# Attention probabilities: from TensorE transposes to VectorE block transposes and a DMA exchange

## The chip, the cores and the metric

One core of one Trainium2 chip. The metric is the device time of the program in microseconds, here the median of three runs; lower is better.

## The reference

One transformer layer on x of 2048 tokens by 512. With 16 heads, NOPE = 128, ROPE = 64, a latent of 128 and causal softmax over all 2048 tokens:

```
xn = layernorm(x)
q = xn @ wq.T                       # per head: 128 plain, 64 rotary
kv_lat, k_pe = split(xn @ wkv_a.T)  # 128 and 64, shared by the heads
kv = rmsnorm(kv_lat, w)
scores = (q_nope @ wkv_b_k @ kv.T + rope(q_pe) @ rope(k_pe).T) * 192**-0.5, causal
out = softmax(scores) @ kv @ wkv_b_v @ wo.T
result = x + out + ternary_linear(xn) + bias
```

## The kernel before, in words

`build_prepare` normalises x, makes the keys (Kn_h, Kn_l, Kp), the values (V_h, V_l), the weights Wq, Wp, Wv of each head, and stores these, the transposed x and the residual in memory. Every float32 operand of a product is split in a high part (a copy rounded to fp32r) and a low part (the difference), and a product of two such operands is three matmuls.

`build_attention` runs over 4 chunks of 512 queries (j) and in each over 16 heads. A chunk j has 4(j+1) units per head; a unit is one score tile of 128 queries by up to 512 keys. A step works on the scores of a head (cur), on the probabilities of the head before (prev) and on the query of the next (nxt). The order on every engine is written out by hand in its `step`.

- TensorE: `scores` (L967, five matmuls of 512 columns, and a mask on the diagonal), `transposes` (L990: for one tile of 128 keys up to four 128x128 transposes of float32 into a ring of three PSUM tiles, L1000), `values` (L1004, three matmuls for one tile of keys, two units behind the transposes), `project_rotary` (12 matmuls, every second head), `project_latent` (12), `project_out` (L1016, 12, at the step's end).
- VectorE: `copy_scores` (L1062: scaled copy of the scores to SBUF with their maximum), `split_tile` (L1077: low part of the transposed probabilities), `rotate`, `split_query`, `split_output`, `accumulate`.
- ScalarE: `exp_row` (L1146, one row of 128 queries at a time), `high_tile` (L1155: high part of the transposed probabilities), `high_output`, `high_query`, `high_rotary`. In a step `high_output` (L1206) stands ahead of the last `exp_row` (L1208).
- GpSimd: `add_rotary` and two halves of `low_rotary` a head.
- SyncE: the loads of Wq, Wp, Wv for coming heads, of xT, tables and residual for the next chunk, and the store of a finished chunk. cosT, sinT and acc have two buffers each, Wq and Wv two.

The probabilities of two heads (probs, 4 rows of 2048 each) are kept.

Of the kernel before, what the change touches and what calls it, by code (L numbers as in the profile page):

```python
# [32 lines left out]
H = 16  # L33
# [18 lines left out]
PT_RING = 3  # L52


def need(eng, sem, value):

    if isinstance(value, int) and value <= 0:
        return
    eng.wait_ge(sem, value)

def heads_before(pos):
    j, m, p = pos
    return H * j + 2 * m + p


def tiles_before(pos):

    j, m, p = pos  # L70
    return QB * H * (j * (j + 1) // 2) + QB * (j + 1) * (2 * m + p)


def rows_before(pos):
    return QB * heads_before(pos)


def pairs_before(pos):
    j, m, p = pos
    return (H // 2) * j + m  # L80


def tiles_of(pos):
    return QB * (pos[0] + 1)


def first_of_chunk(pos):
    return isinstance(pos[1], int) and pos[1:] == (0, 0)


def first_row(pos, k):

    return max(0, k - QB * pos[0])


def rotary_unit(nxt, units):

    if nxt[2]:
        return None
    return units * 3 // 4 if first_of_chunk(nxt) else units // 2 - (1 if units == QB else 0)  # L100


def walk(nc, engine, step):


    def two_steps(j, m):
        step((j, m, 1), (j, m, 0), (j, m + 1, 0))
        step((j, m + 1, 0), (j, m, 1), (j, m + 1, 1))

    for j in range(NCH):  # L110
        step((j, 0, 0), (j - 1, H // 2 - 1, 1) if j else None, (j, 0, 1))
        if j == 0:

            two_steps(0, 0)
        with nc.Fori(0 if j else 1, H // 2 - 1, engines=[engine]) as m:
            two_steps(j, m)
        step((j, H // 2 - 1, 1), (j, H // 2 - 1, 0), (j + 1, 0, 0) if j + 1 < NCH else None)
    step(None, (NCH - 1, H // 2 - 1, 1), None)


def build_prepare(nc, t, keep, stored):
# [4 lines left out]
    with ExitStack() as ctx:  # L126
# [9 lines left out]
        ident, xT, residual = keep["ident"], keep["xT"], keep["acc0"]  # L136
        Wq, Wp, Wv = keep["Wq"], keep["Wp"], keep["Wv"]
# [137 lines left out]
        def _(sp):  # L275
# [51 lines left out]
            rounds(ENG.SP, round_)  # L327

# [462 lines left out]
def build_attention(nc, t, keep, stored):  # L791
    with ExitStack() as ctx:
# [9 lines left out]
        xT, Wq, Wp, Wv = (keep[k] for k in ("xT", "Wq", "Wp", "Wv"))  # L802

        cosT = [keep["cosT"], sb("cosT1", [P, CW])]
        sinT = [keep["sinT"], sb("sinT1", [P, CW])]
        acc = [keep["acc0"], sb("acc1", [P, QB, D])]
# [4 lines left out]
        probs = [sb(f"probs{i}", [P, QB, S]) for i in range(2)]  # L811
        pT_h = [sb(f"pT_h{i}", [P, CW], F32R) for i in range(PT_RING)]
        pT_l = [sb(f"pT_l{i}", [P, CW], F32R) for i in range(PT_RING)]
        o_h = sb("o_h", [P, CW], F32R)
        o_l = sb("o_l", [P, CW], F32R)
        rot_cos = sb("rot_cos", [P, CW])
        rot_sin = sb("rot_sin", [P, CW])
        rotated = sb("rotated", [P, CW])
        part_max = [sb(f"part_max{i}", [P, QB, NCH]) for i in range(2)]
# [3 lines left out]
        ident, ident16, mask = keep["ident"], keep["ident16"], keep["mask"]  # L823
        Kn_h, Kn_l, Kp = (keep[k] for k in ("Kn_h", "Kn_l", "Kp"))
        V_h, V_l = (keep[k][:, :].rearrange("p (n c) -> p n c", c=RANK) for k in ("V_h", "V_l"))

        p_score = [ps(f"p_score{i}") for i in range(2)]
        p_tr = [ps(f"p_tr{i}") for i in range(PT_RING)]
        p_out = ps("p_out")
# [3 lines left out]
        p_result = p_tr + [p_out]  # L833

        xT_in = sem("xT_in")
        tables_in = sem("tables_in")
        wq_in = [sem(f"wq_in{i}") for i in range(2)]
        wp_in = sem("wp_in")
        wv_in = [sem(f"wv_in{i}") for i in range(2)]
# [491 lines left out]
```

## Time and profile before

| What | us |
|---|---|
| median of 3 runs (1955.99 to 1956.75) | 1956.49 |
| the profiled execution | 1956.91 |
| its span | 1955.1 |
| TensorE busy | 1898.6 |
| VectorE busy | 1271.2 |
| ScalarE busy | 889.5 |
| GpSimd busy | 313.3 |

How to read it: one execution was recorded; the span goes from its first to its last instruction. Busy time adds up instructions; a share near 100% marks the engine that has no free time. The chain that ended last goes back from the last instruction, at each step to what released it. PE is TensorE's matmuls, PEld its weight loads, DVE VectorE, ACT ScalarE, POOL GpSimd, SP SyncE; PEclk is TensorE's granted clock as a part of full speed. A stretch is given in us from the span's start. The preparation takes about the first 180 us, the chunks end near 427, 797, 1308 and 1955 us.

### The profile page before, as it was taken

The page shows a single profiled execution, that of the slowest core. Times are in us where ns is not written, and L with a number is a line of the kernel's source. Part 1 is how long each engine was busy: PE and PEld are TensorE (multiplying, and loading weights), DVE is VectorE, ACT ScalarE, POOL GpSimd, SP SyncE. Part 2 cuts the span into 40 slices and gives each one's busy share as a digit, 9 for nine tenths or more (in the row PEclk, how much of TensorE's full clock was granted, in tenths as well). Part 3 has the DMA queues.
Part 4 walks back from the last instruction along what each step waited for, and adds up shares of the span by engine and source line. Part 5 has one row for each costly group of instructions (what it writes and reads, how often), then busy time and mean ns, then how long its engine had stood idle before and what let it go on. Part 6 is the DMA issues. An engine that isn't in the chain of part 4 may idle for free.

```text
span 1955.1 us, 32275 instructions
## 1 busy us (share of the span) xinstructions
PE 1898.6 (97%) x10350; PEld 1586.6 (81%) x10350; DVE 1271.2 (65%) x3025; ACT 889.5 (45%) x1646; POOL 313.3 (16%) x313
## 2 busy tenths in 40 slices
PE   6998999999999999999999999999999999999998
PEld 5887787778888888888888888878888888888886
DVE  4764676766666666666766666666666666666665
ACT  4554444444444444444444444444443444434443
POOL 4773212211111111011100111011010110101100
PEclk9888999999999999999999999999999999999999
DMA  6993322232111112210111101111000110001000
GB/s 207 367 333 149 119 97 81 101 140 87 54 64 54 55 69 101 87 44 35 51 43 43 43 32 54 72 57 45 22 32 32 43 32 21 32 32 43 11 11 22
DMA packets 53077, 147.46 MB, mean 75 GB/s; under 512 B 4835, under 2 KB 17380, under 8 KB 51493
## 3 DMA queue, kind: packets, MB, share of 16 engines
q1 hardware_dynamic: 52208, 145.71, 21.5%
q10 hardware_dynamic: 820, 1.15, 0.2%
q8 instruction: 26, 0.43, 0.1%
q14 instruction: 23, 0.18, 0.0%
HBM read 112.23 MB, written 34.60 MB: 75 GB/s over the span
## 4 chain that ended last, share of the span: by engine, by line
PE 81%; DVE 4%; issue 3%; POOL 2%; ACT 0%; DVEq 0%; POOLq 0%; ACTq 0%
PE p_score L983 31%; PE p_out L1012 18%; PE p_tr L1000 12%; PE p_lat L963 7%; PE p_tr L1023 6%; PE p_rot L963 4%; DVE rot_sin L1095 2%; PE p_out L1023 2%; DVE probs L1068 1%; PE p_score L987 1%; POOL qp_l L1234 1%; POOL qp_l L1237 1%; POOL rotated L1223 1%; DVE pT_l L1080 0%; DVE rot_cos L1091 0%
## 5 line engine op out<-in xcount | busy, mean ns | idle before, releaser
L1160 ACT ACTIVATE pT_h<-p_tr 128x512 fp32r<-128x512 f32 (+3 forms) x640 | 339.4, 532 | 790.4 <-PE p_tr L1000 788.3
L1068 DVE TENSOR_SCALAR_CACHE_REDUCE probs<-p_score 128x512 f32<-128x512 f32 (+3 forms) x640 | 388.3, 607 | 168.8 <-PE p_score L983 109.6
L1080 DVE TENSOR_TENSOR pT_l<-p_tr,pT_h 128x512 fp32r<-128x512 f32 (+3 forms) x640 | 390.2, 610 | 159.9 <-ACT pT_h L1160 153.5
L1000 PE MATMUL p_tr<-ident,probs 128*128 128x128 f32 x2176 | 343.1, 273 | 0.0
L1151 ACT ACTIVATE probs<-probs,neg_max 128x128 f32<-128x128 f32 (+15 forms) x256 | 307.5, 1201 | 70.5 <-DVE neg_max L1074 69.3
L1000 PEld LDWEIGHTS p_tr<-ident,probs 128*128 128x128 f32 x2176 | 260.5, 140 | 52.6 <-issue 0.2
L1012 PE MATMUL p_out<-pT_h,V_h 128*128 128x512 f32 (+3 forms) x640 | 274.7, 429 | 6.8 <-DVE pT_l L1080 6.8
L983 PE MATMUL p_score<-Kn_h,q_h 128*128 128x512 f32 (+3 forms) x640 | 241.4, 377 | 3.3 <-DVE q_l L1102 3.3
L983 PE MATMUL p_score<-Kp,qp_h 128*128 128x512 f32 (+3 forms) x640 | 234.5, 366 | 8.8 <-POOL qp_l L1237 8.8
L1012 PE MATMUL p_out<-pT_h,V_l 128*128 128x512 f32 (+3 forms) x640 | 234.9, 367 | 0.0
L1012 PE MATMUL p_out<-pT_l,V_h 128*128 128x512 f32 (+3 forms) x640 | 233.5, 365 | 0.0
L983 PE MATMUL p_score<-Kp,qp_l 128*128 128x512 f32 (+3 forms) x640 | 233.4, 365 | 0.0
L983 PE MATMUL p_score<-Kn_h,q_l 128*128 128x512 f32 (+3 forms) x640 | 233.4, 365 | 0.0
L983 PE MATMUL p_score<-Kn_l,q_h 128*128 128x512 f32 (+3 forms) x640 | 232.1, 363 | 0.0
L1223 POOL TENSOR_TENSOR rotated<-rot_cos,rot_sin 128x512 f32<-128x512 f32 x32 | 41.1, 1286 | 1112.1 <-DVE rot_sin L1095 1112.1
L963 PE MATMUL p_lat<-xT,Wq 128*128 128x512 f32 x768 | 203.2, 397 | 0.0
L963 PEld LDWEIGHTS p_lat<-xT,Wq 128*128 128x128 f32 x768 | 138.2, 188 | 21.8
L983 PEld LDWEIGHTS p_score<-Kp,qp_h 128*128 128x128 f32 x640 | 120.8, 189 | 29.3 <-POOL qp_l L1237 11.2
L983 PEld LDWEIGHTS p_score<-Kn_h,q_h 128*128 128x128 f32 x640 | 120.8, 189 | 27.3 <-DVE q_l L1102 5.3
L1234 POOL TENSOR_TENSOR qp_l<-rotated,qp_h 64x512 fp32r<-64x512 f32 x64 | 82.4, 1288 | 362.3 <-ACT qp_h L1179 362.3
L983 PEld LDWEIGHTS p_score<-Kn_l,q_h 128*128 128x128 f32 x640 | 121.1, 189 | 22.6
L1117 DVE SCALAR_TENSOR_TENSOR acc<-p_tr,inv_sum,acc 128x512 f32<-128x512 f32 x192 | 132.6, 745 | 8.6 <-PE p_tr L1023 2.8
(138 smaller groups left out, 2622.6 us busy)
## 6 DMA issues: line engine op xcount, KB each, us to landing
Wq<-wq_scr SPq DMA_DIRECT2D x62, 512.0 KB, 3.3
Wv<-wv_scr SPq DMA_DIRECT2D x62, 512.0 KB, 3.3
Wp<-wp_scr SPq DMA_DIRECT2D x31, 512.0 KB, 3.2
wq_scr<-Wq SPq DMA_DIRECT2D x16, 512.0 KB, 5.9
wv_scr<-Wv SPq DMA_DIRECT2D x16, 512.0 KB, 5.8
xT_scr<-xT SPq DMA_DIRECT2D x3, 2048.0 KB, 9.9
xT<-xT_scr SPq DMA_DIRECT2D x3, 2048.0 KB, 7.9
x_in<-in_x SPq DMA_DIRECT2D x4, 1024.0 KB, 7.6
```

The lines of the kernel that those rows point to most:

```text
L963: mm = pe.matmul(out, weights[:, w, it, :], xT[:, x, it, :], start=(it == 0 and k == 0), stop=(it == IT - 1 and k == 2))
L983: mm = pe.matmul(out[:, 0:width], q[p][:, rows], kk[:, keys], start=(k == 0), stop=(k == 4 and b < j))
L1000: mm = pe.transpose(p_tr[k % PT_RING][:, i * P:(i + 1) * P], probs[p][:, i, k * P:(k + 1) * P], ident[:, :])
L1012: mm = pe.matmul(p_out[:, cols], v[:, k, :], pt[r][:, cols], start=(k == 0 and a == 0), stop=(last and a == 2))
L1023: mm = pe.matmul(out[:, :], o[:, rows], Wv[p][:, w, :], start=(k == 0), stop=(k == 2))
L1068: dve.tensor_scalar(probs[p][:, i, b * CW:b * CW + width], p_score[u % 2][:, 0:width], SCALE, LOWEST, ALU.mult, ALU.max, accum_out=part_ma ...
L1080: dve.tensor_tensor(pT_l[r][:, cols], p_tr[r][:, cols], pT_h[r][:, cols].bitcast(F32), ALU.subtract).then_inc(pT_split, 1)
L1117: dve.scalar_tensor_tensor(out=a[:, i, :], in0=p_result[i][:, :], scalar=inv_sum[p][:, i:i + 1], in1=a[:, i, :], op0=ALU.mult, op1=ALU.add ...
L1151: act.activation(probs[p][:, i, 0:width], probs[p][:, i, 0:width], ACT.Exp, bias=neg_max[p][:, i:i + 1], scale=1.0, accum_out=row_sum[p][: ...
L1160: act.activation(pT_h[r][:, cols], p_tr[r][:, cols], ACT.Copy).then_inc(pT_high, 1)
L1223: pool.tensor_tensor(rotated[:, :], rot_cos[:, :], rot_sin[:, :], ALU.add).then_inc(rot_added, 1)
L1234: pool.tensor_tensor(qp_l[p][0:ROPE, :], rotated[own, :], qp_h[p][own, :].bitcast(F32), ALU.subtract).then_inc(qp_ready, 1)
```

## The change

The transposes on TensorE and the splits behind them (`transposes`, `high_tile`, `split_tile`) are gone. In their place:

- VectorE transposes a row of probabilities in blocks of 32x32, up to 8 key tiles in one instruction (`turn_row`), into `turned`; SyncE moves the blocks between the partitions with 16 DMAs a head (`exchange`), each from 32 partitions to 32 partitions, 4(j+1) x 512 bytes in each; ScalarE makes the high parts in groups of two key tiles (`high_group`, a ring of three), GpSimd the low parts, in place (`low_group`). There is one `turned` and one `pT`.
- Step g has the scores of head g, the exchange, groups and values of head g-1 (its last row is turned in step g), the query of head g+1, and output projection and accumulation of head g-2. Except in chunk 0 the values begin at unit 6 (LEAD) and are spread over the units up to the last but one; in chunk 0 they all stand behind the scores.
- The score ring has three PSUM tiles instead of two, the results two; probs keeps three rows. Wq, Wv, cosT, sinT and acc are single. The loops of the sequencers are written out.
- SyncE's order in a step: exchange(g-1), load_q(g+2), load_v(g-1), load_rotary(g+3) in odd steps; tables and xT in step 14 of a chunk, store and load of acc in step 1.

```
+SCORE_RING = 3
+ROW_RING = 3
+HIGH_RING = 3
+LEAD = 6
+def values_by(cur, prev, u):
+    units, tiles = tiles_of(cur), tiles_of(prev)
+    if chunk_of(cur) == 0 or u < LEAD:
+        return 0
+    return min(tiles, -(-tiles * (u - LEAD + 1) // (units - 1 - LEAD)))
+def groups_ahead(cur, prev, u):
+    ahead = min(u + 2, tiles_of(cur) - 1)
+    return (values_by(cur, prev, ahead) + 1) // 2
+def row_due(cur, i):
+    j = chunk_of(cur)
+    return (i + 1) * (j + 1) + (1 if j else 0)
...
+        turned = sb("turned", [P, 4, NT, QB, 32])
+        pT = sb("pT", [P, 4, NT, QB, 32], F32R)
+        pT_h = [sb(f"pT_h{i}", [P, 4, 2, QB, 32], F32R) for i in range(HIGH_RING)]
...
+            def exchange(g):
+                tiles = tiles_of(g)
+                sp.wait_ge(blocked, QB * (g + 1))
+                need(sp, pv_done, tiles_before(g))
...
+                for a in range(4):
+                    for r in range(4):
+                        sp.dma_start(pT[32 * a:32 * (a + 1), r, 0:tiles, :, :].bitcast(F32),
+                                     turned[32 * r:32 * (r + 1), a, 0:tiles, :, :]).then_inc(exchanged, 16)
...
-            def transposes(pos, k):
...
+            def values(g, k):
+                n = groups_before(g) + k // 2
+                if k == 0:
+                    need(pe, o_split, g)
+                if k % 2 == 0:
+                    pe.wait_ge(p_low, n + 1)
...
+                need(pe, accumulated, n - 1)
+                out, rows = p_result[n % 2], slice(i * P, (i + 1) * P)
```

TensorE's step:

```
+                for u in range(units):
+                    if g < HEADS:
+                        scores(g, u)
+                    if u == 0 and g % 2 and g + 1 < HEADS:
+                        project_rotary(g + 1)
+                    if u < QB and g >= 2:
+                        project_out(g - 2, u)
+                    if u < IT and g + 1 < HEADS:
+                        project_latent(g + 1, u)
+                    if 1 <= g < HEADS:
+                        for k in range(done, values_by(g, g - 1, u)):
+                            values(g - 1, k)
```

VectorE's new operation and its step:

```
+            def turn_row(g, i):
+                row, tiles = QB * g + i, QB * chunk_of(g) + i + 1
+                dve.wait_ge(exped, row + 1)
+                if i == 0:
+                    need(dve, exchanged, 256 * g)
+                for first in range(0, tiles, 8):
...
+                    last = dve.transpose(turned[:, :, t8, i, :].rearrange("p a t q -> p t a q"),
+                                         rows.rearrange("p (t a q) -> p t a q", a=4, q=32))
+                last.then_inc(blocked, 1)
...
+                for u in range(units):
+                    if g < HEADS:
+                        copy_scores(g, u)
+                    if 1 <= g <= HEADS and u == (1 if chunk_of(g - 1) else 0):
+                        turn_row(g - 1, QB - 1)
+                    if g >= 2 and u >= 1 and u <= QB - 1:
+                        accumulate(g - 2, u - 1)
...
+                    if u == min(5, units - 1) and g + 1 < HEADS:
+                        split_query(g + 1)
+                    for i in range(QB - 1):
+                        if g < HEADS and u == row_due(g, i):
+                            turn_row(g, i)
+                if 1 <= g <= HEADS:
+                    split_output(g - 1)
+                    invert(g - 1)
```

ScalarE's new operation and its step:

```
+            def high_group(g, k):
...
+                if k == 0:
+                    act.wait_ge(exchanged, 256 * (g + 1))
+                need(act, pv_done, 2 * (n - HIGH_RING + 1))
...
+                for u in range(units):
+                    if 1 <= g < HEADS:
+                        for k in range(done, groups_ahead(g, g - 1, u)):
+                            high_group(g - 1, k)
...
+                    if g < HEADS and (u + 1) % (chunk_of(g) + 1) == 0:
+                        exp_row(g, u // (chunk_of(g) + 1))
+                    if u == 4 and g + 1 < HEADS:
+                        high_query(g + 1)
+                        high_rotary(g + 1)
...
+                if 1 <= g <= HEADS:
+                    high_output(g - 1)
```

GpSimd's step, and the clearing ahead of its first:

```
+                for k in range(groups):
+                    low_group(g - 1, k)
+                    if k == 1 and g + 1 < HEADS:
+                        low_rotary(g + 1, groups_before(g - 1) + 2)
...
+            pool.memset(turned[:, :, :, :, :], 0.0).then_inc(cleared, 1)
```

## Rows read from the trace of the kernel before

**Rows 1.** The page: busy time of the engines; the chain that ended last, by line.
```profile
PE 1898.6 (97%) x10350; PEld 1586.6 (81%) x10350; DVE 1271.2 (65%) x3025; ACT 889.5 (45%) x1646; POOL 313.3 (16%) x313
...
PE p_score L983 31%; PE p_out L1012 18%; PE p_tr L1000 12%; PE p_lat L963 7%; PE p_tr L1023 6%; PE p_rot L963 4%; DVE rot_sin L1095 2%; PE p_out L1023 2%; DVE probs L1068 1%; PE p_score L987 1%; POOL qp_l L1234 1%; POOL qp_l L1237 1%; POOL rotated L1223 1%; DVE pT_l L1080 0%; DVE rot_cos L1091 0%
```

**Rows 2.** Busy time in one stretch: us, then PE, PEld, DVE, ACT, POOL, PEclk, DMA share, GB/s.
```profile
1308.00:1922.00 614.00, 613.09 (x3304) 511.64 (x3303) 396.88 (x928) 275.16 (x420) 45.08 (x35) 1.00 0.09 31
```

**Rows 3.** The chain in order of time, rotary projections: start us, us, what.
```profile
287.25 2.78 PE p_rot L963 x12
...
316.01 2.78 PE p_rot L963 x12
...
488.61 2.76 PE p_rot L963 x12
...
534.01 2.76 PE p_rot L963 x12
...
880.18 2.75 PE p_rot L963 x12
...
943.38 2.75 PE p_rot L963 x12
...
1415.36 2.75 PE p_rot L963 x12
...
1496.98 2.75 PE p_rot L963 x12
```

**Rows 4.** Timeline of PE, chunk 3, first products of two units: start us, us, what.
```profile
1751.08 0.40 PE L983 MATMUL p_score<-Kn_h,q_h 128*128 128x512 f32 x1
...
1753.38 0.40 PE L983 MATMUL p_score<-Kn_h,q_h 128*128 128x512 f32 x1
```

**Rows 5.** Groups by line and form: count, busy us, mean ns, idle before.
```profile
L1000 PE MATMUL p_tr<-ident,probs 128*128 128x128 f32 x2176 | 343.1, 273 | 0.0
...
L1080 DVE TENSOR_TENSOR pT_l<-p_tr,pT_h 128x512 fp32r<-128x512 f32 x448 | 309.3, 691 | 139.1 <-ACT pT_h L1160 134.7
...
L1234 POOL TENSOR_TENSOR qp_l<-rotated,qp_h 64x512 fp32r<-64x512 f32 x64 | 82.4, 1288 | 362.3 <-ACT qp_h L1179 362.3
...
L1080 DVE TENSOR_TENSOR pT_l<-p_tr,pT_h 128x256 fp32r<-128x256 f32 x64 | 27.1, 423 | 10.7 <-ACT pT_h L1160 10.5
...
L1151 ACT ACTIVATE probs<-probs,neg_max 128x1024 f32<-128x1024 f32 x16 | 18.3, 1144 | 1.3 <-DVE neg_max L1074 1.3
...
L336 POOL TENSOR_TENSOR wkb_l<-wkb,wkb_h 128x256 fp32r<-128x256 f32 x16 | 12.3, 768 | 25.4 <-ACT wkb_h L413 25.4
```

**Rows 6.** Timeline of SyncE's queue, chunk 0: start us, us of the issue, what.
```profile
180.60 0.34 SPq L871 DMA_DIRECT2D Wp<-wp_scr  x1
...
197.90 0.43 SPq L894 DMA_DIRECT2D cosT<-in_cosT  x1
198.38 0.43 SPq L895 DMA_DIRECT2D sinT<-in_sinT  x1
```

**Rows 7.** DMA issues: count, KB each, median us to landing.
```profile
Wq<-wq_scr SPq DMA_DIRECT2D x62, 512.0 KB, 3.3
...
xT<-xT_scr SPq DMA_DIRECT2D x3, 2048.0 KB, 7.9
```

**Rows 8.** DMA of 23.93 to 24.48 us, when wqp (64 partitions) lands.
```profile
DMA packets 71, 0.13 MB, mean 231 GB/s; under 512 B 9, under 2 KB 9, under 8 KB 71
```

**Rows 9.** Timelines of DVE and ACT at the end of a chunk-3 step.
```profile
1759.06 0.69 DVE L1068 TENSOR_SCALAR_CACHE_REDUCE probs<-p_score 128x512 f32<-128x512 f32 x1 [1.08 <-PE p_score L987]
...
1761.76 0.69 DVE L1106 TENSOR_TENSOR o_l<-p_out,o_h 128x512 fp32r<-128x512 f32 x1 [1.58 <-ACT o_h L1166]
...
1761.62 2.00 ACT L1151 ACTIVATE probs<-probs,neg_max 128x2048 f32<-128x2048 f32 x1
```

**Rows 10.** Busy time in two stretches of the preparation; columns as in rows 2.
```profile
64.00:68.00 4.00, 2.35 (x17) 1.94 (x14) 3.90 (x6) 0.91 (x2) 2.96 (x3) 0.88 1.08 361
68.00:72.00 4.00, 4.00 (x19) 3.81 (x19) 0.73 (x2) 2.77 (x6) 1.91 (x2) 0.50 1.02 350
```

More of the change, by code:

```diff
@@ L51, with chunk_of, tiles_of, tiles_before @@
 LOWEST = -3.0e38
-PT_RING = 3
-def need(eng, sem, value):
[L57 to L118, printed above, removed]
+SCORE_RING = 3
+ROW_RING = 3
+HIGH_RING = 3
+LEAD = 6
+HEADS = NCH * H
+def need(eng, sem, value):
+    if value > 0:
+        eng.wait_ge(sem, value)
+def chunk_of(g):
+    return g // H
+def tiles_of(g):
+    return QB * (chunk_of(g) + 1)
+def tiles_before(g):
+    j = chunk_of(g)
+    return QB * H * (j * (j + 1) // 2) + QB * (j + 1) * (g - H * j)
+def groups_of(g):
+    return tiles_of(g) // 2
+def groups_before(g):
+    return tiles_before(g) // 2
+def opens_chunk(g):
+    return g % H == 0
+def values_by(cur, prev, u):
[9 more added lines that the diff above has]
+    return (i + 1) * (j + 1) + (1 if j else 0)
 def build_prepare(nc, t, keep, stored):
@@ L855, in build_attention @@
         exped = sem("exped")
[L856 removed]
+        p_high = sem("p_high")
         o_high = sem("o_high")
@@ L1013, in values @@
+                if k % 2 == 0:
+                    pe.wait_ge(p_low, n + 1)
+                last = k == tiles_of(g) - 1
+                i = slice(max(0, k - QB * chunk_of(g)), QB)
+                high, low = pT_h[n % HIGH_RING][:, :, k % 2, i, :], pT[:, :, k, i, :]
+                for a, (v, pt) in enumerate(((V_h, high), (V_l, high), (V_h, low))):
+                    mm = pe.matmul(p_out[:, :, i, :], v[:, k, :], pt, start=(k == 0 and a == 0),
                                    stop=(last and a == 2))
@@ L1022, in project_out, with step @@
                 for k, (o, w) in enumerate(((o_h, 0), (o_h, 1), (o_l, 0))):
-                    mm = pe.matmul(out[:, :], o[:, rows], Wv[p][:, w, :], start=(k == 0), stop=(k == 2))
+                    mm = pe.matmul(out[:, :], o[:, rows], Wv[:, w, :], start=(k == 0), stop=(k == 2))
                 mm.then_inc(out_projected, 1)
-            def step(cur, prev, nxt):
-                units = tiles_of(cur) if cur else tiles_of(prev)
-                tiles = tiles_of(prev) if prev else 0
+            def step(g):
+                units = tiles_of(g) if g < HEADS else QB
@@ L1029, in step @@
                 done = 0
                 for u in range(units):
-                    if cur:
-                        scores(cur, u)
-                    if u < tiles:
-                        transposes(prev, u)
-                    if u >= 2 and u - 2 < tiles:
-                        values(prev, u - 2)
-                        done = u - 1
-                    if nxt and u == rotary_unit(nxt, units):
-                        project_rotary(nxt)
-                order = ["q", "v", "q", "v", "q", "q"] if units == QB else ["q", "v", "v", "q", "q", "q"]
@@ L1043, in step @@
-                it = 0
-                for what in order:
-                    if what == "v" and done < tiles:
-                        values(prev, done)
-                        done += 1
-                    if what == "q" and nxt:
-                        project_latent(nxt, it)
-                        it += 1
-                if prev:
-                    for i in range(QB):
-                        project_out(prev, i)
-            project_rotary((0, 0, 0))
+                    if g < HEADS:
+                        scores(g, u)
@@ new lines, in step @@
+                    if u == 0 and g % 2 and g + 1 < HEADS:
[7 more added lines that the diff above has]
+                            values(g - 1, k)
+                            done = k + 1
+                if 1 <= g <= HEADS:
+                    for k in range(done, tiles_of(g - 1)):
+                        values(g - 1, k)
@@ L1251, in build @@
+            pool.wait_ge(cleared, 1)
+            add_rotary(0)
+            low_rotary(0, 0)
+            for g in range(HEADS + 2):
+                step(g)
 def build(nc, t):
```

430 lines of the change are left out of this document (197 added, 233 removed).

## The prediction

> **What bounds the kernel now.** I read the page first: TensorE is busy 97% of the 1955.1 us span, VectorE 65%, ScalarE 45%, GpSimd 16%, and in the chain that ended last, TensorE's scores are 31% of the span, its values 18%, and the transposes of the probabilities (L1000) 12% [rows 1]. Then the stretch of the last chunk: 613.09 of 614 us busy at full clock, DMA share 0.09 [rows 2]. So TensorE is the bound, and whatever leaves it is gained as long as nothing takes its place. The chain in order of time gives the length of two heads as the distance between two rotary projections: 28.76, 45.40, 63.20 and 81.62 us in chunks 0 to 3 [rows 3], so 14.4, 22.7, 31.6 and 40.8 us a head, 109.5 together; 16 of each are 1752 us of the span. A full unit (five score products, four transposes, three value products) takes 2.30 us from one start to the next [rows 4]; twelve products of that size in a row take 2.75 us [rows 3], 0.23 each, so eight are 1.84 and the four transposes the other 0.46: 0.11 us each.
>
> **What is removed.** 2176 transposes [rows 5] at 0.11 us are 239 us of TensorE; 6.4 us a head in chunk 3 (58 of them), 4.6, 2.9 and 1.1 in the others. VectorE loses 640 splits (390 us), ScalarE 640 copies out of PSUM.
>
> **What is added, and its prices.**
> - VectorE turns each row. Two tensor forms give 0.423 us for 256 and 0.691 for 512 elements [rows 5], 1.05 ns an element over 0.15: 1.22 us for 1024, 2.4 us for a row of 2048. No transpose on VectorE is in the trace; from below, the same at no fixed cost (2.1), from above twice as much. I take 2.4; the upper end adds some 6 us over one head of each chunk, 100 us in all.
> - ScalarE copies groups of two key tiles, 1024 elements: 1.14 us, as the exponential of that width [rows 5].
> - GpSimd now makes the low parts, which VectorE made: 0.768 us for 256 and 1.288 for 512 elements give 2.03 ns an element, 2.33 us for 1024; the last group of a head is half, 1.3. Beside it stay two rotary lows of 1.29 [rows 5] and, every second head, an add of the same length. In chunk 3 that is 7 × 2.34 (with the wait) + 1.3 + 2.6 = 20.3 us behind the exchange.
> - SyncE issues 16 DMAs a head, 1, 2, 3 or 4 MiB in all. Issues behind one another stand 0.48 us apart, of which the issue itself is 0.43; alone it takes 0.34 [rows 6]; I take 0.43 (0.34 to 0.48): 6.9 us before the last has started, whatever its size. 512 KB land in 3.3 and 2048 KB in 7.9 us [rows 7]: 342 GB/s over 1.8 us. But these reach all 128 partitions, each exchange DMA reads 32 and writes 32. The nearest row is a load to 64 partitions, at 231 GB/s [rows 8]. I take 230, nearest in shape; 342 is the upper end, and the lower 156, if a quarter of the partitions falls behind a half as the half does behind the whole (231/342).
>
> The Trainium skill, SBUF — State Buffer, section Door 1: The DMA port swizzle, says that 32 partitions reach 8 of 16 ports, some 218 GB/s, and that two DMAs to different halves do not add up; by it the sum below would be some 35 us larger; it gives 64 partitions no more than 32, and the row's 231 GB/s is near its figure.
>
> So the exchange X (issue or bytes, whichever is longer, plus 1.8) is 8.7, 10.9, 15.5 and 20.0 us in chunks 0 to 3.
>
> **What it costs depends on what stands in series with it.** Nothing is doubled: one turned tile, one pT. The exchange of head g−1 can't start before its last row is turned, early in step g; turn_row(g, 0), in the middle of VectorE's queue, waits for it, and the score copies behind it, so the score ring stops TensorE; and the values need GpSimd's lows, which need it too. I follow chunk 3 from the last score product of a step:
> - Copy and maximum 1.1 us, exponential of 2048 elements 2.1, then high_output, which is queued behind that exponential, 0.6, then split_output 0.7 [rows 9]: only at 4.7 may TensorE project out. That, three latent products and scores(1) take 2.5 us, the copy 0.75, and VectorE, in whose queue turn_row(g−1, 3) stands behind this copy, ends it at 8.0 + 2.4: D = 10.6 us.
> - X = 20.0. TensorE has done all score units up to 6 by about 18 us and waits.
> - From the landing: high group 1.2, low group 2.4, and then TensorE's values (0.69 us a full tile) and scores (1.15) as the lows come: low 2 stands behind the rotary lows at 10.9, and with 13 us of values and scores behind, TensorE ends scores(15) 26.4 us after the landing.
> The head is 10.6 + 20.0 + 26.4 = 57.0 us against 40.8. The others by the same walk:
> - Chunk 2 (12 units): a shorter exponential and row make D = 9.6; behind the landing two high groups, the query's and the rotary's copies and GpSimd's lows (3.6, 5.9, rotary to 8.5, then 10.8, 13.2, 15.5, 16.8 us) decide, with values 8 to 11 and the last two scores behind them: 20.2. 9.6 + 15.5 + 20.2 = 45.3 for 31.6.
> - Chunk 1 (8 units): D = 7.8; all eight values stand in unit 6, the fourth high group waits for the first two values (ring of three), the rotary copies stand behind it, so the rotary lows end at 10.4, the last low at 14.0, and two values and scores(7) follow: 16.0. 7.8 + 10.9 + 16.0 = 34.7 for 22.7.
> - Chunk 0 (4 units): turn_row(g, 0) is in unit 1, so behind the landing come VectorE's last two units with accumulates and, every second head, rotary (3.2 or 4.6 us to the last maximum), the exponential 0.9, the query's copy 0.6, a high group 1.2, lows and rotary lows 6.2 (scores of the next head wait for these), then score, copy and the turn of the last row 1.9, and in odd steps 0.8 more for the add: 15.1 with the waits. 15.1 + 8.7 = 23.8 for 14.4.
> Sum 160.8 for 109.5: 51.3 × 16 = 821 us more. So the transposes' 239 us are inside and paid over.
>
> Loads of Wq, Wv and Wp now stand behind the exchange on SyncE. They are for the next step and land in 3.3 us [rows 7]; a step leaves 15 us or more after the exchange, so I count nothing; without that cover, 3 us a head. Single acc, tables and xT cost at chunk ends up to 10 us each, against a last step whose values and outputs are shorter without transposes; the clearing of turned, once, is 8192 elements, at most 16.6 us by GpSimd's slope, partly beside the first rotary: 0 in sum, bounds ±30.
>
> **The clock.** After a stretch with TensorE busy 2.35 of 4 us, its granted clock was 0.50 (1.2 GHz) through the next 4 us, which it worked without a gap [rows 10]. The change makes a gap of over 10 us a head. At 1.2 GHz some 3 us can be lost behind each; most of it lies under GpSimd's lows. Bounds 0 and 192 us, taken 1 us a head: 64.
>
> The sum is made against the execution's own 1956.9 us (span 1955.1), which is 0.4 us above the median of the runs: 1957 + 821 + 64 = 2840 us.
>
> **Rivals.**
> 1. The exchange runs as fast as a transfer over all partitions, 342 GB/s: X = 8.7, 8.7, 11.0, 14.1, and 38.7 × 16 + 64 = 683: 2640 us. For it: SBUF to SBUF takes no memory access outside, and the sources alternate. Against it: [rows 8]. 0.20.
> 2. The clock stays down behind the gap through the whole tail, where TensorE works only as lows come. At 1.2 GHz its 19.8 us of values and scores in chunk 3 become 39.6 for 26.4, and 26 for 20.2 in chunk 2: 19 × 16 = 304 more, 3080 us. Against it: once it is the slower one it has no gaps, and where the trace shows none for long the clock is whole [rows 2]. 0.14.
> 3. On the other side: the exchange is hidden, as the late values intend. Its place is the wait of turn_row(g, 0); it decides below X = 3.8 us in chunk 3 (37.0 + X = 40.8) and is fully hidden near 2 us, below which TensorE sets the end: 1957 − 239, and back 2.3, 1.9, 1.5 us a head for the output split behind the exponential (91 us): 1810 us. It needs 4 MiB at over 1000 GB/s, or my series is not one. 0.04, and 0.01 for ending within the measurement.
> 4. The change doesn't keep what it says: the transposes do leave, but "late in a step" is no cover if everything before unit 6 takes 18 us and the landing comes at 30. That is inside the forecast.
>
> The Trainium skill, TensorE: Matmul & The Clock Gate, section HAM oscillation, describes a kernel that is thrown back to the low clock at every wait for a DMA; here that is rival 2 where it lasts, and the 64 us of my sum where not.
>
> **How the numbers follow.** The forecast (exchange at 190 to 260 GB/s, 2740 to 2980) has 0.61. With rivals 1 and 2 in part the range is 2570 to 3040: below it lie the fast exchange with cheap issues and rival 3, above it the clock that stays down, and 156 GB/s (some 310 us more). Over 0.2% (4 us, about what a measurement of this kernel can tell) slower 0.95, faster 0.04, same 0.01.
>
> **What would show it.** Right: TensorE busy at some 60%, one long idle time a head, ended in the waits by p_low, o_l or q_l; VectorE's longest wait for the exchange before a transpose; SyncE's 16 issues some 0.4 us apart in each head; GpSimd busy about 1000 us; periods near 48, 69, 91 and 114 us for two heads; the last exchange of a head landing 20 us after its first issue in chunk 3. Wrong: DMA moving over 300 GB/s within an exchange (rival 1), clock near 0.5 in the value stretches (2), or values beginning at unit 6 with no wait (3). A transpose on VectorE of 2.4 us for 1024 elements would put the end about 100 us later.

## The result, and the profile after

The changed kernel takes 3007.3 us (median of four runs, 2998.91 to 3010.15), against 1956.62 for the kernel before: 1.536 times as long, with a 95% interval of 1.533 to 1.540. The forecast was 2840 (2570 to 3040), slower. So the sign and the range held; the move was forecast as +883 us and is +1051, 168 more. The profiled execution took 3010.1 us, with a span of 3007.9.

The page, first engines and TensorE's granted clock in 40 slices:

```profile
PE 1929.9 (64%) x8174; PEld 1539.6 (51%) x8174; DVE 1209.3 (40%) x2769; ACT 857.6 (29%) x1326; POOL 1000.7 (33%) x634
...
PEclk9987677688877877878797888878878888788877
```

Against [rows 1] TensorE has 2176 instructions fewer, and is busy 64% of the time for 97%. It is no longer the bound, and no other engine is: the next, VectorE, is busy 40%. That is the picture of work in series. The waits say which series (what waited <- for what: us in total, times, longest):

```profile
POOL pT L1244 <- ACT pT_h L1165: 1221.5, 73, 41.9
...
PE p_out L1006 <- POOL pT L1244: 853.1, 113, 22.8
...
ACT pT_h L1165 <- DMA pT<-turned: 626.6, 49, 25.2
...
DVE turned L1073 <- DMA pT<-turned: 359.0, 48, 16.1
```

Read upwards from the DMA: ScalarE's first copy of a head waits for the exchange (49 times 12.8 us), GpSimd for ScalarE, TensorE for GpSimd. In chunk 0, where ScalarE does not wait, VectorE does. One head of chunk 3, put together from the timelines of SyncE, ScalarE, GpSimd and TensorE (start us, us, what; in brackets the idle time before it and what ended it):

```profile
2599.14 14.99 SPq L876 DMA_DIRECT2D pT<-turned  x16
2614.16 1.17 SPq L882 DMA_DIRECT2D Wq<-wq_scr  x1
...
2621.29 1.06 ACT L1165 ACTIVATE pT_h<-pT 128x1024 fp32r<-128x1024 f32 x1 [16.90 <-DMA pT<-turned]
...
2622.42 2.36 POOL L1244 TENSOR_TENSOR pT<-pT,pT_h 128x1024 fp32r<-128x1024 f32 x1 [40.00 <-ACT pT_h L1165]
...
2624.93 0.77 PE L1006 MATMUL p_out<-pT_h,V_h 128*128 128x512 f32 x1 [18.03 <-POOL pT L1244]
...
2630.59 13.07 POOL L1244 TENSOR_TENSOR pT<-pT,pT_h 128x1024 fp32r<-128x1024 f32 x6
```

The 16 issues alone take 15 us, and the first copy starts 22.15 us after the first issue; TensorE stands still for 18 us, up to the first low part. GpSimd is busy from 2622.42 to 2643.66 almost without a gap: that is the series of low parts behind the landing. The same head in stretches of 5 us (columns as in [rows 2]):

```profile
2600.00:2605.00 5.00, 5.00 (x26) 4.17 (x26) 2.45 (x8) 1.78 (x2) 0.00 (x0) 1.00 0.97 213
2605.00:2610.00 5.00, 1.90 (x9) 1.25 (x7) 1.65 (x5) 0.00 (x0) 0.00 (x0) 0.96 1.04 215
2610.00:2615.00 5.00, 0.00 (x0) 0.00 (x0) 0.00 (x0) 0.00 (x0) 0.00 (x0) 0.50 1.01 210
2615.00:2620.00 5.00, 0.00 (x0) 0.00 (x0) 0.00 (x0) 0.00 (x0) 0.00 (x0) 0.50 1.01 203
2620.00:2625.00 5.00, 0.07 (x1) 0.10 (x1) 2.14 (x3) 3.65 (x5) 2.36 (x1) 0.50 0.59 208
2625.00:2630.00 5.00, 5.00 (x15) 4.13 (x16) 1.61 (x6) 2.48 (x4) 4.51 (x3) 0.50 0.00 0
```

For ten microseconds no engine works at all and the DMA engines move 203 to 210 GB/s at a share of 1.0: they are full, at that rate. The Trainium skill, SBUF — State Buffer, section Door 1: The DMA port swizzle, gives 218 GB/s for 32 partitions; the trace agrees, at 5% less.

The length of a head is the distance of the output split (L1106 before, L1100 after) from one head to the next, X the time from the first issue of an exchange to its last landing; both are means over the same 12 heads in the middle of each chunk:

| chunk | before | after | forecast | X after | X forecast |
|---|---|---|---|---|---|
| 0 | 14.39 | 27.47 | 23.8 | 11.6 | 8.7 |
| 1 | 22.74 | 39.23 | 34.7 | 12.0 | 10.9 |
| 2 | 31.68 | 47.96 | 45.3 | 17.3 | 15.5 |
| 3 | 40.55 | 60.55 | 57.0 | 22.4 | 20.0 |
| sum | 109.4 | 175.2 | 160.8 | 63.3 | 55.1 |

Sixteen of each: 65.8 × 16 = 1053 us, the whole of the move.

### The profile page after: what moved, and what is told of

The parts are those of the page before. It is cut to its first block and busy times, and to the rows that moved or that the text cites. A ratio compares the mean times of both kernels' runs of the same rounds, so it can differ in the third digit from the quotient of the medians.

```text
span 3007.9 us, 24655 instructions
## 1 busy us (share of the span) xinstructions
PE 1929.9 (64%) x8174; PEld 1539.6 (51%) x8174; DVE 1209.3 (40%) x2769; ACT 857.6 (29%) x1326; POOL 1000.7 (33%) x634
## 5 line engine op out<-in xcount | busy, mean ns | idle before, releaser
L1244 POOL TENSOR_TENSOR pT<-pT,pT_h 128x1024 fp32r<-128x1024 f32 x320 | 682.8, 2159 | 1228.1 <-ACT pT_h L1165 1221.5
L1006 PEld LDWEIGHTS p_out<-pT_h,V_h 128*128 128x128 f32 x640 | 156.1, 244 | 928.5 <-issue 741.1
L1165 ACT ACTIVATE pT_h<-pT 128x1024 fp32r<-128x1024 f32 x320 | 301.9, 967 | 893.3 <-DMA pT<-turned 626.6
L1073 DVE STREAM_TRANSPOSE turned<-probs 128x1024 f32<-128x1024 f32 (+7 forms) x384 | 341.8, 916 | 359.1 <-DMA pT<-turned 359.0
L1018 PE MATMUL p_result<-Wv,o_h 128*128 128x512 f32 x512 | 194.4, 464 | 172.7 <-DVE acc L1114 93.1
L1006 PE MATMUL p_out<-pT_h,V_l 128*128 128x512 f32 (+3 forms) x640 | 283.9, 444 | 0.0
L1006 PE MATMUL p_out<-pT,V_h 128*128 128x512 f32 (+3 forms) x640 | 281.2, 439 | 0.0
L1018 PEld LDWEIGHTS p_result<-Wv,o_h 128*128 128x128 f32 x512 | 90.9, 209 | 213.1 <-DVE acc L1114 108.1
L1114 DVE SCALAR_TENSOR_TENSOR acc<-p_result,inv_sum,acc 128x512 f32<-128x512 f32 x256 | 188.7, 739 | 3.1 <-PE p_result L1018 2.4
L1006 PEld LDWEIGHTS p_out<-pT,V_h 128*128 128x128 f32 x640 | 156.0, 244 | 27.5
```

Source lines behind the costliest of these rows:

```text
L1006: mm = pe.matmul(p_out[:, :, i, :], v[:, k, :], pt, start=(k == 0 and a == 0), stop=(last and a == 2))
L1018: mm = pe.matmul(out[:, :], o[:, rows], Wv[:, w, :], start=(k == 0), stop=(k == 2))
L1073: last = dve.transpose(turned[:, :, t8, i, :].rearrange("p a t q -> p t a q"), rows.rearrange("p (t a q) -> p t a q", a=4, q=32))
L1114: dve.scalar_tensor_tensor(out=acc[:, i, :], in0=p_result[(QB * g + i) % 2][:, :], scalar=inv_sum[g % 2][:, i:i + 1], in1=acc[:, i, :], op ...
L1165: act.activation(pT_h[n % HIGH_RING][:, :, :, i, :].rearrange("p r t i q -> p r t (i q)"), pT[:, :, tiles, i, :].bitcast(F32).rearrange("p ...
L1244: pool.tensor_tensor(low, low.bitcast(F32), high.bitcast(F32), ALU.subtract).then_inc(p_low, 1)
```

## The experiments

Each ran once, with a profile, beside the kernel before at 1955.95 to 1956.89 us; four repeats of the changed kernel spread over 11 us, so differences under some 12 us are not read. All edits are to the changed kernel. Four head lengths in a row are those of chunks 0 to 3, and these and every X are means over the 12 heads of the table; the texts put down before the runs took X from one head of each chunk (11.9, 12.6, 17.4 and 22.1).

**One DMA of the sixteen.** The exchange moves a sixteenth; the rest of pT keeps zeros, so fifteen sixteenths of the probabilities are left out of the values.

```
-                for a in range(4):
-                    for r in range(4):
-                        sp.dma_start(pT[32 * a:32 * (a + 1), r, 0:tiles, :, :] ...
+                sp.dma_start(pT[0:32, 0, 0:tiles, :, :] ... turned[0:32, 0, 0:tiles, :, :]) ...
```

> Leaves out fifteen of the sixteen DMAs of every exchange (only the block from partitions 0 to 31 to partitions 0 to 31 is moved; the rest of pT stays cleared); all waits stay. Series theory (the whole exchange stands in every head's chain): the exchange takes 11.9, 12.6, 17.4 and 22.1 us in chunks 0 to 3 of the changed kernel, and one DMA about 2.4, so each head loses 9.5, 10.2, 15.0 and 19.7 us, 16 times 54.4 = 870 us of 3007: about 2140 us, some 50 less if TensorE's clock stays up. Rival (VectorE's transposes or GpSimd's lows are the bound and the exchange lies beside them): above 2700 us.

Measured 2361.38 us; heads 22.44, 31.89, 36.24 and 44.3, 40.3 less in sum. SyncE's and ScalarE's timelines:

```profile
2070.01 0.51 SPq L874 DMA_DIRECT2D pT<-turned  x1
...
2075.15 1.04 ACT L1162 ACTIVATE pT_h<-pT 128x1024 fp32r<-128x1024 f32 x1
```

X is 2.0, 2.3, 2.6 and 3.0 us now, so it falls by 9.6, 9.8, 14.6 and 19.4 us; the heads fall by 5.0, 7.3, 11.7 and 16.3 us, that is 2.4 to 4.6 us less in each chunk. In chunk 3 the first copy starts 5.1 us after the issue, behind an exponential, with no wait for a DMA. So the first few microseconds of an exchange lie beside work that has to be done anyway, in every chunk, and below that other work sets the head. 646 us of the 1051 go with the fifteen DMAs, together with what their wait did to TensorE's clock (a mean of 0.895 now, for 0.813); the 405 that are left (2361 against 1956) come with no exchange worth the name. I had expected X to count whole and missed by some 220 us.

**Sixteen small DMAs.** All are issued, but each moves one tile of keys, 16 KB in every chunk; the other key tiles of the probabilities are left out.

```
-                        sp.dma_start(pT[32 * a:32 * (a + 1), r, 0:tiles, :, :] ...
+                        sp.dma_start(pT[32 * a:32 * (a + 1), r, 0:1, :, :] ...
```

> All sixteen DMAs of an exchange, but each moves one key tile only (512 bytes of each of 32 partitions; the rest of pT stays cleared). Issue theory (SyncE's issues of 0.65 us each set the exchange where the data are few): the exchange is 16 times 0.65 plus 1.5 = 11.9 us in every chunk, so the others lose 0.7, 5.5 and 10.2 us a head, 262 us: 2745 us. Rival (bytes alone at some 205 GB/s): a quarter of a MiB is moved in under 2 us, the exchange takes about 3.5 us, 50 us less over the four chunks' heads: 2200 us.

Measured 2724.57 us; heads 27.22, 38.17, 42.21, 49.56. SyncE's and ScalarE's timelines in chunk 3:

```profile
2438.01 10.01 SPq L876 DMA_DIRECT2D pT<-turned  x16
...
2449.26 1.06 ACT L1165 ACTIVATE pT_h<-pT 128x1024 fp32r<-128x1024 f32 x1 [5.05 <-DMA pT<-turned]
```

With hardly any bytes the 16 issues take 10 us, 0.63 each, and the landing follows 11.25 us behind the first. Chunk 0 is as slow as with all bytes (27.22 for 27.47), chunk 3 is 11 us faster. So issues bound chunk 0 and nearly all of chunk 1, bytes chunks 2 and 3. In these two X falls by 5.9 and 10.9 us and the head by 5.8 and 11.0: at this size the exchange counts whole.

**Alternating halves.** The order of the 16 DMAs changes, so that neighbours write to and read from different halves of the partitions.

```
-                for a in range(4):
-                    for r in range(4):
+                for s in range(4):
+                    for q in range(4):
+                        a, r = (0, 2, 1, 3)[q], (0, 2, 1, 3)[(q + s) % 4]
```

> The same sixteen DMAs in another order: neighbours write, and read, alternately partitions 0 to 63 and 64 to 127. Theory of the halves (a transfer to 32 partitions reaches half of what SBUF can take, and a queue of transfers to both halves gets more): the exchange in chunks 2 and 3 falls from 17.4 and 22.1 us to the issue's 12 to 13, 14 us less, 16 times: about 2785 us. Rival (the rate is that of each DMA by itself, whatever stands beside it): no change, 2995 to 3020 us.

Measured 2951.01 us, neither of the two; X is 20.5 in chunk 3 and 15.4 in chunk 2, 1.9 us less in both, and so are the heads (58.67 and 46.10). In stretches within an exchange:

```profile
2560.00:2565.00 5.00, 0.55 (x3) 0.13 (x1) 0.29 (x2) 0.00 (x0) 0.00 (x0) 0.91 1.02 233
2565.00:2570.00 5.00, 0.00 (x0) 0.00 (x0) 0.00 (x0) 0.00 (x0) 0.00 (x0) 0.50 1.02 231
```

The rate rises from some 207 to 232 GB/s, an eighth: the order counts, but sixteen transfers in a queue do not overlap enough to make up one over all partitions, which the loads of [rows 7] show at 342.

**Last row turned first.** VectorE turns the last row of the head before it copies any score of the step.

```
                 for u in range(units):
+                    if 1 <= g <= HEADS and u == 0:
+                        turn_row(g - 1, QB - 1)
                     if g < HEADS:
                         copy_scores(g, u)
-                    if 1 <= g <= HEADS and u == (1 if chunk_of(g - 1) else 0):
-                        turn_row(g - 1, QB - 1)
```

> VectorE turns the last row of head g-1 as the first thing of step g, ahead of both score copies, instead of behind the second. Series theory: the exchange starts earlier by the two copies and the wait for the second scores, 4.9, 3.6, 2.9 and 0.3 us in chunks 3 to 0, 11.7 times 16 = 187 us less: 2820 us. Rival (the start of the exchange is not on the path that sets the end): 3000 us or more, since the copies that free the score ring come later.

Measured 2825.11 us, 182 less; heads 27.31, 36.23, 43.84, 56.33. The turn no longer stands behind two copies and the wait for the second scores, and the first issue comes 2.9, 4.2 and 4.4 us sooner behind the last exponential in chunks 1 to 3. The heads are 3.0, 4.1 and 4.2 us shorter, so all of that is gained: the start of the exchange is on the path.

**Two issuing queues.** ScalarE issues the half that writes partitions 64 to 127, behind its first work of a step.

```
-                for a in range(4):
+                for a in range(0, 2):
...
+            def exchange_part(g):
+                act.wait_ge(blocked, QB * (g + 1))
+                need(act, pv_done, tiles_before(g))
+                for a in range(2, 4):
+                    for r in range(4):
+                        act.dma_start(pT[32 * a:32 * (a + 1), r, 0:tiles, :, :] ...
```

> The changed kernel, with the 16 DMAs of an exchange issued half by SyncE and half by ScalarE. It tells the cost of issuing from the cost of the bytes with all bytes kept. Theory (issues at 0.65 us each bound chunks 0 and 1, bytes at 207 GB/s bound chunks 2 and 3): first issue to landing falls from 11.9 to about 7 us in chunk 0, from 12.6 to 11.9 in chunk 1, and stays at 17.4 and 22.1 in chunks 2 and 3; 6 us over the four chunks, times 16 is 96: about 2910 us. Rival a (the rate belongs to one queue, two carry twice as much): chunk 3 near 14 us, together 23 us, 2640 us. Rival b (issues hold each other up across queues): no change, 2995 to 3015 us.

Measured 2901.02 us. X is 6.9, 11.4, 16.9 and 21.6 us in chunks 0 to 3, forecast 7, 11.9, 17.4 and 22.1. The timelines of SyncE and ScalarE in chunk 3:

```profile
2495.30 14.15 SPq L876 DMA_DIRECT2D pT<-turned  x8
...
2495.30 15.58 ACTq L1166 DMA_DIRECT2D pT<-turned  x8
2510.98 1.68 ACT L1154 ACTIVATE probs<-probs,neg_max 128x1664 f32<-128x1664 f32 x1 [23.62 <-issue]
```

The queues run side by side, but with bytes in the way eight issues take as long as sixteen did: 1.8 and 1.9 us each. An issue's length in chunks 2 and 3 is the DMA engines' pace, handed back to the queue. The Trainium skill, DMA: Bandwidth & Descriptors, section Rules for kernel authors, says that spreading DMAs over issuing engines only saves issue time; the run agrees: of its 106 us 80 lie in chunk 0 (22.48 us a head for 27.47), where issues were the bound. X is also 0.4 to 0.8 us shorter in chunks 1 to 3; why was not separated. The second queue has a price on ScalarE, whose exponential of the next row stands behind the issues.

**The clock held.** Idle products into the output bank that the values overwrite, placed where TensorE waits for the first low part.

```
                     need(pe, o_split, g)
+                    for _ in range(16 * chunk_of(g)):
+                        pe.matmul(p_out[:, :, :, :], Kn_h[:, 0:P], Kn_l[:, 0:CW], start=True, stop=True)
```

> The changed kernel, with 16, 32 and 48 idle products (128x512, into the output bank that the values overwrite) a head in chunks 1, 2 and 3, placed where TensorE waits for the first low parts; they take 3.7, 7.4 and 11 us at full clock, less than the waits of 8.6, 13.2 and 18.0 us there. They keep TensorE's clock from falling and measure what its fall costs. Theory (my term of 1 us a head, on 48 heads): about 2950 us. Rival a (the slow values lie wholly under GpSimd's low parts): 2995 to 3010. Rival b (the clock costs 3 us a head): about 2860 us, with the values behind the wait at 0.23 us each instead of 0.43.

Measured 3025.65 us, above all that was expected. In chunk 3 the 48 products left a gap of 7 us, and the values began at 0.43 us each, at a granted clock of 0.50 again. So the run tells little of the clock, and a longer one followed, `(0, 32, 50, 72)[chunk_of(g)]` in place of `16 * chunk_of(g)`:

> The changed kernel with more idle products than e6_warm (32, 50 and 72 a head in chunks 1 to 3: 7.4, 11.5 and 16.6 us at full clock, against waits of 8.6, 13.2 and 18.0 us), since in that run 48 left a gap of 7 us in chunk 3 and the values began at 0.43 us each, at a granted clock of 0.50. Theory (now the fall is gone, but its cost was under GpSimd's lows): values at 0.23 us each from the first, time 3000 to 3035, as e6_warm. Rival (the fall of the clock costs what I forecast, and e6_warm did not prevent it): about 2950.

Measured 3016.23 us; the mean granted clock rises from 0.813 to 0.913. The page's clock row:

```profile
PEclk9887776799999899999999999999999999999998
```

From the ninth slice on, chunk 1 and later, it is 9 tenths or more in nearly every one, for the 7s and 8s of the changed kernel. One head of it in stretches, the values starting at 2619.20 (columns as in [rows 2]):

```profile
2610.00:2615.00 5.00, 5.00 (x24) 4.14 (x23) 0.00 (x0) 0.00 (x0) 0.00 (x0) 1.00 0.99 201
2615.00:2620.00 5.00, 3.33 (x15) 2.42 (x14) 2.79 (x4) 4.31 (x6) 2.75 (x2) 1.00 0.48 186
2620.00:2625.00 5.00, 4.33 (x21) 3.19 (x19) 1.04 (x6) 4.33 (x5) 4.65 (x4) 1.00 0.00 0
2625.00:2630.00 5.00, 2.64 (x6) 2.12 (x7) 0.61 (x2) 0.06 (x1) 5.00 (x3) 0.74 0.01 2
```

The clock holds over the landing and the first values take 0.23 us each, yet the time does not fall. TensorE, faster now, runs into GpSimd's low parts (POOL 4.65 and 5.00 of 5 us busy) and waits there, and the values behind that wait take 0.43 us each again:

```profile
2627.36 0.74 PE L1008 MATMUL p_out<-pT_h,V_h 128*128 128x512 f32 x1 [2.49 <-POOL pT L1246]
```

The heads show what the total hides: 27.39, 38.13, 48.62 and 61.94 us, so 1.1 less than in the changed kernel in chunk 1, and 0.7 and 1.4 more in chunks 2 and 3. In chunks 2 and 3 the last low part ends 17.2 and 22.6 us behind the landing, for 17.1 and 22.3 without the idle products: their pace there is GpSimd's, whatever TensorE's speed, and behind later waits TensorE loses what it had gained: the last score ends 0.7 us later in both. In chunk 1 they end 1.2 us sooner, because ScalarE's fourth high group waits for the first two values. The exchange is also longer beside the idle products, 23.0 us for 22.4 in chunk 3, and 22.9 with fewer of them; why is open. So this run moves the fall of the clock to a later wait; what a clock that never falls would be worth, it doesn't measure.

**Output first.** On top of the last row turned first (2825 us), ScalarE copies the output's high part before the last exponential of the step, in chunks 1 to 3.

```
+                    early = 1 <= g < HEADS and chunk_of(g) > 0
+                    if early and u == units - 1:
+                        high_output(g - 1)
                     if g < HEADS and (u + 1) % (chunk_of(g) + 1) == 0:
                         exp_row(g, u // (chunk_of(g) + 1))
...
-                if 1 <= g <= HEADS:
+                if 1 <= g <= HEADS and not early:
                     high_output(g - 1)
```

> The kernel with the last row turned first in a step (2825 us), and besides, in chunks 1 to 3, the output's high part made by ScalarE ahead of the last row's exponential, so that TensorE and VectorE needn't wait for it behind that exponential. Theory (the exchange's start sets the head: it comes 1.1 us earlier, as copy and split of the output leave the path between exponential and turn): 48 x 1.1 = 53 us, about 2770 us. Rival a (TensorE's own early work is in the series too): the 2.2 us of both count, about 2720. Rival b: hidden, 2815 to 2830.

Measured 2771.46 us, 54 less for 53 forecast; heads 27.12, 35.25, 42.70, 55.15, about 1.1 less each in chunks 1 to 3. Only what stands between the last exponential and the first issue counts.

**All four together** (turned first, output first, two queues, halves alternated in both).

> The four edits that give the exchange less to wait for together: last row turned first, output's high part ahead of the exponential, issues on two queues, and partition halves alternated in both. If their gains add (182 + 53 + 96 + 56 us): about 2620 us. Theory (exchange stays in series with the lows, so still far above the kernel before): 2600 to 2720 us. Rival (shorter exchanges fall under the 4 us of other work that the kernel with one DMA showed, so the gains overlap): 2720 to 2780 us.

Measured 2626.33 us. The plain addition of what each gave (182, 54, 106 and 56 us) makes 2609, so the gains add but for 17 us; the 2620 expected had 96 us for the two queues. Heads 22.49, 34.07, 40.90, 53.55. It is the fastest variant of the changed kernel that leaves nothing out, and still 670 us above the kernel before.

**Low parts split.** VectorE makes every second low part, with a semaphore of its own; it stands in VectorE's queue at the end of the unit before the one whose values need it.

```
+                dve.tensor_tensor(low, low.bitcast(F32), high.bitcast(F32), ALU.subtract).then_inc(p_low_v, 1)
...
-                    pe.wait_ge(p_low, n + 1)
+                    pe.wait_ge(p_low_v if n % 2 else p_low, n // 2 + 1)
...
                 for k in range(groups):
+                    if k % 2 == 0:
                         low_group(g - 1, k)
```

> The changed kernel, with every second low part made by VectorE (1.2 us each by its slope) and the others by GpSimd (2.36 us each). It measures how much of a head is GpSimd's series behind the landing. Theory (the series is the bound): in chunk 3 four lows and two rotary lows instead of eight and two leave TensorE's own 19.8 us as the bound, 3.8 us less a head; by the same walk about 5, 4 and 2.4 us less in chunks 2, 1 and 0; together 15 x 16 = 243: about 2760 us. Rival a (high parts and TensorE at its low clock take the place of the lows): 2890 to 2960. Rival b (VectorE's lows delay the copies of the scores as much as they give): 2990 to 3020.

Measured 3057.25 us, 50 slower: neither the theory nor rival a, and beyond rival b. Heads 27.27, 40.11, 49.18, 61.71. VectorE's and GpSimd's timelines in chunk 3:

```profile
2671.20 1.22 DVE L1084 TENSOR_TENSOR pT<-pT,pT_h 128x1024 fp32r<-128x1024 f32 x1
2676.53 2.76 DVE L1084 TENSOR_TENSOR pT<-pT,pT_h 128x1024 fp32r<-128x1024 f32 x1
...
2671.59 3.09 POOL L1263 TENSOR_TENSOR pT<-pT,pT_h 128x1024 fp32r<-128x1024 f32 x1 [1.21 <-ACT pT_h L1184]
2675.81 2.40 POOL L1263 TENSOR_TENSOR pT<-pT,pT_h 128x1024 fp32r<-128x1024 f32 x1 [1.13 <-ACT pT_h L1184]
```

VectorE's part starts first at 2671.20 and takes 1.22 us, up to 2672.42; GpSimd's, begun at 2671.59, ends at 2674.68, 2.26 us after that end. The other way round GpSimd's ends at 2678.21 and VectorE's, begun at 2676.53, 1.08 us after. So the two did not run beside each other, they took turns; over all its 96 parts of this width VectorE needs 2.15 us on average. The Trainium skill, SBUF — State Buffer, section Who interferes with whom, states this as a lock between a VectorE instruction with two inputs in SBUF and a reading GpSimd one; the trace agrees. On top of that VectorE's part stands behind score copies and a turn of 2.1 us, and GpSimd now waits, 1.21 and 1.13 us in these rows, for ScalarE's high parts, which wait for the values three groups back (237 us in this kernel, 266 in the changed one). In this head the last low part ends 22.1 us after the first high part began (in the changed kernel 22.4), but over 12 heads it ends 19.2 and 23.5 us behind the landing in chunks 2 and 3, for 17.1 and 22.3: halving GpSimd's share made the series longer. Which of the turns and the two queues weighs how much was not separated.

**Low parts split, and the clock held.**

> e9_low_split and e10_warm_long together: with fewer lows on GpSimd nothing should hide the slow products. Theory (the clock's cost was hidden by the lows, some 2.5 us a head where it shows): some 120 us below e9_low_split. Rival (the clock costs nothing there either): within 20 us of e9_low_split.

Measured 2996.79 us, 60 below the split alone: half of what I expected and outside the rival. Heads 27.40, 38.60, 47.78, 61.29: the clock held over the landing is worth 1.5 and 1.4 us a head in chunks 1 and 2 and 0.4 in chunk 3.

**All five.**

> The kernel with the four edits for the exchange (2626 us), and every second low part on VectorE. Theory (exchange and lows are in series, so the gains add): 2626 less what e9_low_split gives (forecast 243), about 2390 us, still some 430 us above the kernel before, of which 22 to 40 us a head of exchange and turning in series are the cause. Rival (the two shorten each other's cover): 2450 to 2600.

Measured 2675.83 us, 50 above the four together, where I had expected about 2390, and 2450 to 2600 as the rival. The split costs the same there as alone.

## Why the prediction was right, and where it was off

The direction is right for the reason given: with one buffer the exchange, the turn before it and the lows behind it stand in series. That the time lies in the range owes something to luck: 3007 is above the band of 2740 to 2980 that had 0.61, and 33 us below the upper end, in a part of the range that was meant for rivals 1 and 2 in part. What brought the time there are three terms that the sum had too small: the issue, the rate, and the tail of chunk 1. By the parts of a head, in us, forecast in brackets (D from a head's last score to the first issue, the tail from the landing to the next head's last score; in chunk 0, where the parts lie otherwise, the head without X):

| chunk | D | X | tail |
|---|---|---|---|
| 0 | together 15.9 (15.1) | 11.6 (8.7) | |
| 1 | 7.6 (7.8) | 12.0 (10.9) | 19.7 (16.0) |
| 2 | 10.2 (9.6) | 17.3 (15.5) | 20.6 (20.2) |
| 3 | 11.1 (10.6) | 22.4 (20.0) | 27.3 (26.4) |

- **TensorE leaves the bound, and a series takes its place.** Right: 60% busy forecast and 64% found. The longest wait in front of a value is for GpSimd's low part, as said, and VectorE's longest wait for the exchange stands before a turn. The transposes' 239 us were not tried by themselves; they can't show, since TensorE no longer sets the end.
- **Turn, high and low parts.** 2.37 us for a row of 2048 (forecast 2.4), 1.06 for a high part (1.14) and 2.36 to 2.38 for a low one (2.33); GpSimd busy 1000.7 us for about 1000. Slopes from [rows 5] held within 8%.
- **The issue, mis-sized.** I took 0.43 us from loads of weights and tables [rows 6]. The exchange's issues behind one another take 0.64 us in chunk 0 and 0.63 with a quarter of the bytes; one alone takes 0.51. So 16 are 10.2 us, not 6.9: X is 2.9 us too short in chunk 0, and in chunk 1, where two queues brought X from 12.0 to 11.4, 0.6 of its 1.1. In chunks 2 and 3 issues take 0.70 and 0.94 us because the engines are full, as the two queues showed. I also chose the short rows: at the start of the same trace loads issued behind one another take 0.39 to 0.71 us each, as this one does.

```profile
2.76 0.64 SPq L280 DMA_DIRECT2D wkb<-in_wkv_b  x1
```

- **The rate, mis-sized.** 230 GB/s was taken, from [rows 8]; 203 to 215 were measured. 4.19 MB at 207 are 20.3 us instead of 18.2: +2.1 of the 2.4 in chunk 3, and by the same rate +1.5 of the 1.8 in chunk 2. Together X is 8.2 us over four heads too short, 131 of the missing 168 us. The 218 GB/s of the Trainium skill (SBUF — State Buffer, Door 1: The DMA port swizzle) would have put the forecast 35 us nearer. 342 GB/s, rival 1, is excluded by the windows.
- **The tail in chunk 1, mis-sized.** X taken off, 111.9 us are left over the four heads for the 105.7 I had, 99 us in all against the 64 that I gave the clock. More than half of it is in chunk 1, whose tail is 3.7 us too short. One head there, from the timelines of ScalarE and TensorE and in one stretch (columns as in [rows 2]):

```profile
1018.98 0.63 ACT L1165 ACTIVATE pT_h<-pT 128x512 fp32r<-128x512 f32 x1 [3.62 <-PE p_out L1006]
...
1026.61 0.80 PE L1006 MATMUL p_out<-pT_h,V_h 128*128 128x512 f32 x1 [6.21 <-POOL pT L1244]
...
1027.00:1032.00 5.00, 5.00 (x16) 4.34 (x16) 0.00 (x0) 0.00 (x0) 0.78 (x1) 0.50 0.00 0
```

The walk had the order right: the fourth high group waits for the first two values. But it took these and the last two values at full speed. The last low part ends 15.3 us behind the landing for 14.0, and then values and the last scores take 4.3 us for 2.0, at a mean granted clock of 0.61, with nothing beside them but the end of the last low part.

- **The clock, partly hidden.** The fall is there (0.50 through the wait and the first values). In chunks 2 and 3 it lies under GpSimd's lows, as I had written for "most of it". In chunk 1 it doesn't: held over the landing it gave 1.1 us a head, and behind the second wait some 1.7 more can be lost, an estimate (4.3 us at a mean clock of 0.61, less what they would take at 1.00). So 1 us for every head was an even spread of a cost that sits mostly in chunk 1; that the whole was of the right order is luck. Rival 2, the clock down through the whole tail, came true in chunk 1, which it had not priced: 0.62 on average from the landing to the last score, for 0.82 and 0.86 in chunks 2 and 3, where the clock is whole again after the first values. What fills the other 0.8 to 1.2 us a head in chunks 0, 2 and 3 was not traced to one instruction.
- **"X counts whole".** Right at its size, as the small DMAs, the alternated halves and the two queues show (in chunk 0 X fell by 4.8 us there and the head by 5.0), wrong further down. With one DMA I expected 2140 us and 2361 was measured, because the first 2.4 to 4.6 us of an exchange have cover. This touches rival 3: I had put a hidden exchange at 1810 us. The kernel with hardly any exchange is at 2361, so what stands before the first issue and behind the landing costs over 400 us without it; 236 of the changed kernel's microseconds went with the last row turned first and the output first.
- **The loads behind the exchange.** Costed at nothing. Wq is issued at 2614.16, 15 us behind the first exchange DMA, and no wait for Wq, Wv or Wp by TensorE's scores, values or projections is in the trace. Right.
- **The sum.** 821 + 64 = 885 forecast for the heads and their clock; measured 65.8 × 16 = 1053. Of the 168, 131 are X (issues (2.9 + 0.6) × 16 = 56, the other 75 mostly the rate), and 35 what the fixed parts took beyond the 64.

## What to carry to other kernels

Before a transpose is taken off the bounding engine, draw the chain that replaces it for one head and add up its parts in series: with one buffer, the wait for a transfer stops the producer and the consumer both, and "late in a step" hides only what fits before the first use. Price a transfer by its own shape: here 16 issues over 32 partitions took 0.64 us each and moved 207 GB/s, where the kernel's other loads show 0.34 to 0.71 us and 342 GB/s. And before work is moved to an idle engine, ask what its queue holds at that moment and whether the two engines can work side by side: half of GpSimd's work on a VectorE that was busy 40% made the kernel 50 us slower.

## What was not expected of the hardware

- The length of an issue is no constant: 0.51 us alone, 0.63 to 0.64 in a row of 16, 0.94 with the DMA engines full, and 1.8 to 1.9 on each of two queues that feed them together.
- The order of DMAs with 32 partitions each matters within one queue: alternating the halves raised the rate from some 207 to 232 GB/s and took 56 us off the kernel.
- A VectorE subtraction with both inputs in SBUF took 1.22 us where it began first and 2.76 where GpSimd's had begun before it; GpSimd's went from 2.36 to 3.09 the other way round.
- A mean granted clock of 0.913 for 0.813 did not shorten the kernel: chunk 1 gained 1.1 us a head, chunks 2 and 3 lost 0.7 and 1.4.
